# A fused embedding, sequence-filter and attention kernel: small loads behind the text rows, normed rows on two 64-partition sections, projections on both, bias added by VectorE

## The reference

```python
h = tok(x, W)                       # edge pad, patches of 16 with step 8, rfft, product with W.T
h = concat([h, txt(x_txt, ...)])    # 1024 + 77 = 1101 rows: tree embedding looked up by x_txt
h = h + attn(layernorm(h), ...)     # "attn": a long convolution over the rows, gelu, W_fc, gelu, + input, layernorm
h = h + ffn(layernorm(h), ...)      # below
# ffn, 4 heads n, 4 experts e, head dimension 16
sx = x @ hl_w[n].T + hl_b[n]                       # (b, 4, rows, 16)
q = sx @ wq[n, e].T;  k = sx @ wk[n].T;  v = sx @ wv[n].T
att = softmax(q @ k.T * 4 + causal);  out = att @ v
mixed = sum_e(out[e] * softmax_e(out @ gate_w + gate_b))
hn = layernorm(mixed + sx[n, n])
fout = layernorm(fc2(relu(fc1(hn))) + hn)          # inside each head
return fout * softmax_n(fout @ fgate_w.T)
```

## Time and profile before

| what | value |
|---|---|
| median of 3 runs | 1377.04 us (1374.37 to 1379.66) |
| the profiled execution's own time | 1382.09 us |
| its span, first to last instruction | 1379.2 us |
| mean granted TensorE clock | 0.893 |
| busy share of the span: PE, DVE, ACT, POOL | 79%, 57%, 55%, 32% |
| front stage, from the span's start | 0 to 186 us |
| sequence stage | 186 to 373 us |
| first prologue | 373 to 442 us |
| period 0 | 442 to 565 us |
| six full periods, period 7, last epilogue | 565 to 1221, to 1320, to 1379 us |

### The profile page before, as it was taken

One profiled execution on the slowest core, in us unless ns is written; L12 is line 12 of the kernel. 1 busy time (PEld: TensorE's weight loads), 2 busy tenths in 40 slices (PEclk: granted clock), 3 DMA queues, 4 the chain that ended last, 5 costly groups with the idle time before them and its releaser, 6 DMA issues.

```text
span 1379.2 us, 39174 instructions
## 1 busy us (share of the span) xinstructions
PE 1091.8 (79%) x15223; PEld 596.9 (43%) x15223; DVE 793.0 (57%) x1493; ACT 754.5 (55%) x906; POOL 443.6 (32%) x616
## 2 busy tenths in 40 slices
PE   3898628889052699989989889879989898989931
PEld 2455327775021345444444444444434444534411
DVE  3828675325756274267567558448567656752453
ACT  0242114452001565867867877866876786789820
POOL 3000031001520431243543543525444435355431
PEclk9999859995555798999999999999999999999965
DMA  8999049940406507404603612620830740550000
GB/s 147 214 170 240 11 104 202 203 79 1 103 21 116 76 15 138 65 4 109 108 9 99 109 19 78 99 53 15 152 60 15 135 77 14 113 91 3 3 17 10
DMA packets 114013, 113.69 MB, mean 82 GB/s; under 512 B 68072, under 2 KB 85239, under 8 KB 113669
## 3 DMA queue, kind: packets, MB, share of 16 engines
q1 hardware_dynamic: 109776, 110.59, 42.3%
q10 hardware_dynamic: 3733, 0.60, 0.3%
q0 software_dynamic: 320, 0.04, 0.0%
HBM read 88.07 MB, written 22.95 MB: 81 GB/s over the span
## 4 chain that ended last, share of the span: by engine, by line
PE 42%; issue 11%; ACT 9%; DVE 6%; POOL 3%; ACTq 0%; DMA 0%; POOLq 0%; DVEq 0%; SPq 0%
PE b_pso L1986 15%; PE b_pss L1950 13%; ACT b_pb L2065 9%; PE b_psm L2012 4%; PE b_pss L1948 3%; POOL b_pb L2103 2%; PE b_psm L2008 2%; PE b_psm L2029 2%; POOL b_stat L2084 1%; DVE b_rq L2191 1%; PE b_psm L1932 1%; DVE b_ks L2189 1%; PE b_psm L2033 1%; DVE b_squares L2190 1%; PE b_psm L2034 1%
## 5 line engine op out<-in xcount | busy, mean ns | idle before, releaser
L2065 ACT ACTIVATE b_pb<-b_pss 128x1024 f32<-128x1024 f32 (+2 forms) x736 | 648.4, 940 | 295.7 <-PE b_pss L1950 221.7
L1986 PE MATMUL b_pso<-b_pb,b_vop 128*32 128x128 f32 (+4 forms) x4800 | 407.3, 415 | 28.6 <-POOL b_pb L2103 28.5
L2103 POOL TENSOR_SCALAR_AFFINE_SELECT b_pb<-b_pb 128x256 f32<-128x256 f32 (+1 forms) x544 | 253.4, 487 | 495.5 <-ACT b_pb L2065 492.6
L1950 PE MATMUL b_pss<-b_qop,b_kop 97*32 97x512 bf16 (+3 forms) x6144 | 354.4, 333 | 52.3 <-issue 31.0
L1950 PEld LDWEIGHTS b_pss<-b_qop,b_kop 97*32 97x32 bf16 x6144 | 140.3, 96 | 274.9 <-ACT b_pb L2065 156.0
L1986 PEld LDWEIGHTS b_pso<-b_pb,b_vop 128*32 128x32 f32 x4800 | 159.7, 112 | 109.9 <-issue 39.5
L2279 DVE STREAM_TRANSPOSE b_ot<-b_pso 128x512 f32<-128x512 f32 x64 | 45.9, 717 | 133.5 <-PE b_pso L1986 131.1
L2084 POOL TENSOR_TENSOR b_stat<-b_stat,b_mh 128x18 f32<-128x18 f32 x34 | 110.2, 3259 | 30.2 <-DVE b_stat L2358 18.8
L920 PE MATMUL psc<-tz,ub 128*64 128x128 f32 x1152 | 79.8, 283 | 16.2 <-ACT tz L961 8.8
L920 PEld LDWEIGHTS psc<-tz,ub 128*64 128x64 f32 x1152 | 71.5, 141 | 24.5 <-ACT tz L961 12.7
L2012 PE MATMUL b_psm<-b_xt,w_all 65*128 65x384 f32 x144 | 63.4, 562 | 18.9 <-DVE b_rq L2191 16.4
(11 more groups left out here) (394 smaller groups left out, 1308.9 us busy)
## 6 DMA issues: line engine op xcount, KB each, us to landing
b_qop<-qk_parts_b SPq DMA_DIRECT2D x192, 144.0 KB
tz<-taps SPq DMA_DIRECT2D x64, 304.0 KB, 9.6
x<-in_x SPq DMA_DIRECT2D x16, 1024.0 KB, 14.6
qk_parts_b<-b_qs SPq DMA_DIRECT2D x16, 864.0 KB, 5.3
b_kop<-qk_parts_b SPq DMA_DIRECT2D x192, 36.0 KB
qk_parts_b<-b_ks SPq DMA_DIRECT2D x8, 432.0 KB, 3.9
n_late<-id_d SPq DMA_DIRECT2D x1, 2400.0 KB, 9.4
h<-z SPq DMA_DIRECT2D x8, 288.0 KB, 2.8
```

Source lines behind the costliest of these rows:

```text
L1950: mm = pe.matmul(pss[VW * g:VW * g + VW, u % 2, b, col:col + w], lhs, qop[:, n, e, q0:q0 + w], start=True, stop=True, skip_group_check=True)
L1986: mm = pe.matmul(acc, vop[0:P if j < NA - 1 else LAST, j, n, :], rhs, start=(j == 0), stop=(q0 == P * j if x < 2 else j == NA - 1), skip_g ...
L2065: nc.scalar.activation(pb[:, SLOT[un], 0:nb, 0:w], pss[:, s % 2, 0:nb, 0:w], ACT.Exp, scale=float(HD) ** 0.5).then_inc(exped, 1)
L2103: ins = pool.affine_select(out=v_, in_=v_, compare_op=ALU.is_ge, fill=0.0, base=0, pattern=pat, channel_multiplier=-1)
```

## The change

1. **Front, SP's queue.** The 32 small loads L303 and L308 are issued behind the text rows and behind the store of the taps.
2. **Sequence stage.** The copy `ul` moves from POOL to ScalarE. POOL's addition to `hh` waits until the convolution is over (`psw_out` 3). `w_all` gets 128 rows: its 64 weight rows twice (from `whad`, wha's columns twice). The bias row becomes two tiles, `vb` (v and residual bias in every partition, made by TensorE with `whab`) and `bcol` (q and k bias by column), copied by VectorE. The gate product moves to the fifth of the 16 groups; the wait for the last group moves behind the first bias matmul.
3. **FFN, two sections.** `xt` is [128, 576]: positions 0 to 575 on partitions 0 to 63, 576 to 1151 on 64 to 127. Each product is a pair of matmuls with 64 contracted rows, one on each half of the array's rows, into different banks. "feat" becomes 6 jobs of 2 x 288 positions instead of 5 (of them one half job) with 9 x 384; "tok" and "rmat" are 8 blocks of 128 and two of 64. VectorE adds the bias as it takes a job out. A prologue has 10 jobs instead of 9, and FULL_STEPS (VectorE's steps in a full period) is 96 instead of 87.
4. **Slots.** PRO, EPI, XNORM, CHECK and BOUND get the slots in the diff: the norm of the next rows stands at slot 0 instead of 9, its turn at 11 instead of 21.
5. **First prologue.** `run(-1)` uses three PSUM areas in turn, so TensorE may be two jobs ahead of VectorE; "tok" is last. The k parts of head 0 are copied back by ScalarE's queue, as soon as k is spilled; `run(0)` starts scores when all jobs of it are given free.
6. **End.** The flag is computed during the last epilogue and stored before the last output.

```diff
@@ front, SP @@
                 small_weights()
-                gate_weights()
...
                 sp.dma_start(krev_d, kr).then_inc(kr_stored, 16)
+                block_weights()
+                gate_weights()
@@ sequence stage @@
+                pe.matmul(psf[:, 1, 0:NH * VC], whad[:], w.wvx[:].rearrange("p n c -> p (n c)"), start=True, stop=True)
+                pe.matmul(psf[:, 1, NH * VC:2 * NH * VC], whab[:], w.wvx[:].rearrange("p n c -> p (n c)"), start=True, stop=True)
...
-                pool.tensor_copy(ul[:], ut[:].rearrange("p d a b -> p (a b) d")).then_inc(ul_ok, 1)
-                pool.wait_ge(ul_ok, 1)
+                pool.wait_ge(psw_out, 3)
                 pool.tensor_tensor(hh[:], hh[:], bmid(w.lnb[:], NG), ALU.add).then_inc(hl_ok, 1)
@@ FFN stage @@
+        PRO = [(11, "turn", 0), (15, "tok", 0), (19, "feat", (2, 0)), (24, "feat", (2, 1)), (30, "knorm", 0), (33, "feat", (0, 0)), (37, "feat", (0, 1))]
+        PRO += [(41, "feat", (1, 0)), (46, "feat", (1, 1)), (50, "qnorm", 0)]
+        EPI = [(55, "fc1", 0), (58, "fc2", 0), (61, "back", 0), (64, "back", 1)]
...
-        CHECK, BOUND = 25, 51
-        FXNORM, XNORM, LASTNORM = (11, (28, 31), 36), (9, (11,), 14), (71, (74, 76), 80)
+        CHECK, BOUND = 17, 53
+        FXNORM, XNORM, LASTNORM = (11, (28, 31), 36), (0, (5,), 8), (71, (74, 76), 80)
+        FIRST = [(11, "turn", 0)] + [j for j in PRO if j[1] not in ("turn", "tok")] + [(56, "tok", 0)]
+        def area(p, i):
+            return (psm[:], pss[:, 0], pss[:, 1])[i % 3] if is_first(p) else psm[:]
@@ SP, ACT: first prologue @@
+                        if not att:
+                            sp.wait_ge(keys_out, 1)
...
+                    if not att and pro:
+                        act.wait_ge(spilled, 32)
+                        act.sem_inc(keys_out, 1)
+                        for i, kp in enumerate(TERMS_K):
+                            act.dma_start(kop[HD * i:HD * i + HD, 0], qk_d[0, kp, 2 * P:2 * P + HD]).then_inc(placed[0], 16)
@@ PE, fill @@
                     elif kind == "feat":
-                        gate(base)
-                        for i, (g, x) in enumerate(c):
-                            mm = pe.matmul(psm[:, i, 0:FB], wall[:, g * P:g * P + P], xt[:, x * FB:(x + 1) * FB], start=True, stop=True)
+                        psm = gate(base, p, kind)
+                        g, i = c
+                        for h in range(2):
+                            r = slice(D * h, D * h + D)
+                            mm = pe.matmul(psm[:, h, 0:PIECE], wall[r, g * P:g * P + P], xt[r, PIECE * i:PIECE * i + PIECE], start=True, stop=True)
@@ DVE, empty, a q job (FEAT) @@
-                        ch.step(cp(dst(0), psm[0:m, 0:z, 0:FB]))
-                        ch.step(tt(squares[0:m, slot[c[0]]:slot[c[0]] + z, :], dst(0), dst(0), ALU.mult))
-                        give(tt(rq[0:m, 0:z], psm[0:m, 0:z, 0:FB], dst(0), ALU.subtract))
+                            ch.step(ts(dst(0), psm[:, :, 0:PIECE], bcol[:, g:g + 1], None, ALU.add))
+                            ch.step(tt(cut(sqq[:, g, :]), dst(0), dst(0), ALU.mult))
+                            give(stt(rest, psm[:, :, 0:PIECE], bcol[:, g:g + 1], dst(0), ALU.add, ALU.subtract))
@@ DVE, norms @@
                         if att and not prev and s == RNORM[2]:
-                            v.wait_ge(rstd, roots0 + 2)
+                            v.wait_ge(rstd, roots0 + 3)
```

More of the change, by code:

```diff
@@ L1705, in stage_ffn_bounded @@
     UB, PB, LAG = 2, 5, 3
+    HALF, PIECE = LP // 2, LP // 4
+    MIDDLE = NA // 2
+    BLOCKS = [(a + 5 * h, h, P * (a + 5 * h) - HALF * h, P, 0) for a in range(MIDDLE) for h in range(2)]
+    BLOCKS += [(MIDDLE, 0, P * MIDDLE, P // 2, 0), (MIDDLE, 1, 0, P // 2, P // 2)]
     units = score_units(UB, whole_tiles=True)
@@ L1845, in _, with copies @@
                     sp.sem_inc(s_, c)
-                def copies(c, n):
+                def copies(c, n, keys=True):
                     qk, mt_ = qk_d[c], mt_d[c]
@@ L1921, in job, with gate, turn_rows @@
                     k[0] += 1
-                def gate(base):
-                    pe.wait_ge(free, base + k[0] + 1)
-                def turn_rows(src, base):
-                    gate(base)
+                def gate(base, p, kind):
+                    if is_first(p):
+                        need = {"turn": 1, "feat": 2, "tok": 2, "knorm": 4, "qnorm": k[0] + 1}[kind]
+                        pe.wait_ge(free, max(need, k[0] - 1))
+                    else:
+                        pe.wait_ge(free, base + k[0] + 1)
+                    return area(p, k[0])
+                def turn_rows(src, base, p, kind):
+                    psm = gate(base, p, kind)
                     pe.sem_inc(passed, 1)
@@ L1996, in fill @@
                         pe.wait_ge(rn_ok, 1)
-                        turn_rows(h4[:, NA * c:NA * (c + 1)], base)
+                        turn_rows(h4[:, NA * c:NA * (c + 1)], base, p, kind)
                         return
                     if kind == "rmat":
-                        gate(base)
-                        for a in range(NA):
-                            mm = pe.matmul(psm[:, 0, a * HD:(a + 1) * HD], xt[:, a * P:(a + 1) * P], wall[:, WC + HD * c:WC + HD * c + HD], start=True, stop=True)
+                        psm = gate(base, p, kind)
@@ new lines, in fill @@
+                        for a, h, c0, n, off in BLOCKS:
+                            r = slice(D * h, D * h + D)
+                            if n == P:
+                                o = NH * VC * (a % 5)
+                                mm = pe.matmul(psm[:, h, o:o + NH * VC], xt[r, c0:c0 + n], wall[r, WV:], start=True, stop=True)
+                            else:
+                                for z in range(2):
+                                    mm = pe.matmul(psm[off:off + n, z, 4 * NH * VC:TOK], xt[r, c0:c0 + n], wall[r, WV + NH * VC // 2 * z:WV + NH * VC // 2 * (z + 1)], start=True, stop=True)
+                    elif kind == "feat":
+                        psm = gate(base, p, kind)
+                        g, i = c
+                        for h in range(2):
+                            r = slice(D * h, D * h + D)
+                            mm = pe.matmul(psm[:, h, 0:PIECE], wall[r, g * P:g * P + P], xt[r, PIECE * i:PIECE * i + PIECE], start=True, stop=True)
@@ L2041, in run @@
                         pe.wait_ge(late_ok, 2)
+                        pe.wait_ge(free, len(PRO) + 1)
                     for s in range(SPAN):
@@ L2115, in run @@
                                 root(variances(p) + norms, st, i * m, (i + 1) * m)
+                        if not att and prev and s == REDUCE:
+                            pool.wait_ge(flag_ready, 1)
+                            pool.partition_all_reduce(bad[:, 1:2], bad[:, 0:1], channels=P, reduce_op=RMAX).then_inc(bad_ready, 1)
                     if not att and not prev:
@@ L2196, in empty @@
-                        if c == ((2, 2),):
-                            ch.step(red(nearest[D:P, 3:4], nearest[D:P, 0:4], AX.X, ALU.min))
+                            rest = rq[0:D]
+                            give(ts(rq[:], psm[:, :, 0:PIECE], bcol[:, 2:3], None, ALU.add))
+                            v.wait_ge(free, base + k[0] + 1)
+                            if i == 0:
+                                ch.done(red(nearest[D:P, 0:2], rq[D:P], AX.X, ALU.min, apply_absolute_value=True))
+                            else:
+                                ch.done(red(nearest[D:P, 2:3], rq[D:P, 0], AX.X, ALU.min, apply_absolute_value=True))
+                                ch.done(red(nearest[D:P, 3:4], rq[D:P, 1, 0:L - 3 * PIECE], AX.X, ALU.min, apply_absolute_value=True))
```

184 lines of the change are left out of this document (109 added, 75 removed).

## The result

The changed kernel takes 1320.78 us, median of 4 runs (1311.28 to 1330.65), against 1377.53 for the one before in the same comparison: ratio 0.959 with a 95% interval of 0.9505 to 0.9676, so 56.8 us or 4.1% faster. The forecast was 1333.5 (-43.6), in a range of 1314 to 1358. Two later comparisons gave 1319.06 (ratio 0.9558, 0.9514 to 0.9601) and 1317.99 (0.9534, 0.9503 to 0.9565). The profiled execution took 1314.63, its span is 1312.2; against the 1379.2 of before that is -67.0, more than the medians show: the profiled execution of before took 4.6 us more than its median, that of the changed kernel 6.2 less.

The account below looks back on a forecast made before the run. Limits taken: late text rows (front), DMA (convolution), a TensorE-VectorE chain (first prologue), TensorE (full periods). Terms -7.7 - 2.9 - 0.5 - 12.5 + 7.5 - 27 - 0.5 = -43.6 gave 1333.5 us, range 1314 to 1358.

Parts of the forecast that it names:

- Rival 4: Period 0: no stall, since TensorE runs ahead with scores and full tiles; 1321 us, chance 10%.
- Front, convolution, fold: Text rows issued earlier, -7.7 us; taps arriving steadily, -2.9; gate product off the path between fold and W_fc, -0.5.
- First prologue: Three areas leave only VectorE's part, q ready 10.8 us earlier; fewer key copies on SP's queue, 1.7; sum -12.5.
- Scores start near 429.7: End of the first prologue: first scores at 429.7 instead of 442.26.
- Pairs: Full periods: both halves run together, a feat job 0.75 us instead of 1.49, tok 1.45 instead of 2.42.
- rival 1: Feat, tok, rmat: halves don't run together, feat pair 1.2 us, tok 2.3; +22 and +6 us, 1361, chance 8%.
- Rival 2: Tok and rmat: only the loads go in turn, tok saves 0.3 us instead of 0.95; +7, 1340.5, chance 10%.
- +7.5: Period 0, net us: late rows and residual norm stall TensorE; shorter rmat (3.2) and feat, tok, waits (4.0) come off.
- The +13.0: Period 0: masks behind POOL's roots go on 41.1 us after the first scores instead of 28.1.
- Full periods: Six periods: shorter feat and tok, less waiting for POOL, minus 1.3 us at the turn; -4.5 each, -27 in all.
- Rivals 3 and 5: Full periods: (3) VectorE's slot-0 wait holds TensorE, 1395 us, 4%; (5) `xn` 2 to 3 us after slot 11, 1348, 13%.
- The end: Tail: flag arithmetic, POOL's reduction and the last DMA leave it, -0.5 us.

Follow-up runs that it names:

- the variant on one half: Changed kernel with both matmuls of every feat, tok and rmat pair contracting rows 0 to 63, so they cannot run side by side: 1352.98 us in one run.

## Why the prediction was right or wrong

The time lies in the range, 12.7 us under the forecast of 1333.5. In the profile the kernel gained 23.4 us more than the sum has: 10.7 of it in period 0, 9.3 in the W_fc products and 5.0 in the full periods, with the other parts 1.6 the other way. Rival 4 names the very time (1321 for 1320.78), but its mechanism is not there: the stall came, so that agreement is luck.

**Front, convolution, fold: right in the profile, less sure than it looks.** -7.15, -2.9 and -0.7 for -7.7, -2.9 and -0.5. Undoing the order of the small loads brings the 7.7 us wait back. But the front takes 178.9 to 182.4 us in the 12 profiles that have the new order, 4.7 to 8.2 less than the one profile of before, and the convolution 103.6 to 105.6 in all 13 profiles with the change, 1.7 to 3.7 less. No run undoes the changes to the convolution by themselves. ScalarE's copy of `ul` took 8.55 us, above the 4 to 8 of the forecast.

**First prologue: right in size, the cause named wrong.** -12.7 for -12.5 (-11.7 to -12.7 in the three profiles), and the keys' queue gives about 2 where the sum had 1.7. VectorE's part is as forecast, 3.5 us for a q job (379.89 to 383.38) where the sum had 3.3. But "with three areas only VectorE's part stays" names the wrong cause: with one area only 2 to 3 us come back. What is left, some 8 us, can only be put down to "tok" going last and pairs of 1.33 us at half clock instead of jobs of 2.92, which fit into VectorE's own time. That is argued, not shown: no run undoes either. "Scores start near 429.7" counts the prologue alone; with the front and the sequence stage the same sum gives 418.7. They started at 409.46, 32.8 us earlier than before where the signs had 23 to 25, and 9.3 of that are the W_fc products.

**Pairs: right.** 0.69 and 1.46 us for 0.75 and 1.45, and the variant on one half shows that it is the halves: 1.17 and 2.35, as rival 1 had (1.2 and 2.3). Rival 1 would have cost more than forecast, though: that variant is 38 us longer in its span than the second profile of the changed kernel (1350.9 to 1312.8), not 28. Rival 2 is out with "tok" at 1.46: 16 loads of 128 columns and 8 of 64 start within it. An estimate by what the Trainium skill, "TensorE: Matmul & The Clock Gate", section "LDWEIGHTS (loading the stationary operand)", gives for one load puts them at 2.1 us one after another. That fits the 2.35 of the variant on one half and not the 1.46 on two, so on different rows they overlap.

**Period 0: a stall, but on another path and of another size, and the sum wrong.** The step that failed is "**+7.5**", in three places. First the path. The +13.0 is the time by which POOL's masks go on later (41.1 for 28.1), and POOL's roots did end there, at 449.93, 40.5 us after the first scores. But TensorE did not wait for the masks. Its longest wait in the first 20 slots, in the changed kernel and then in the one before:

```profile
PE b_psm L1976 <- DVE b_xn L2417: 21.1, 1, 21.1
```

```profile
PE b_pso L1986 <- POOL b_pb L2103: 8.1, 1, 8.1
```

TensorE stood at the turn, now in slot 11, for `xn`, which came 34.5 us after the first scores; no wait for POOL is on its list for period 0. Second the size. At slot 20 period 0 was 14.2 us behind the one before, close to the +14.7 of the sum, but by luck: 4.6 of it are the turn, "tok" and the first "feat" (2.44, 1.46 and 0.69 us on TensorE), which stand ahead of slot 20 now and stood behind it before. The stall itself cost 9.6. Third, from slot 20 to its end the period won 17.4 us: 3.6 in the four "rmat" jobs (0.89 each for 0.8), 7.1 in the other jobs (2.5 net of the 4.6 moved ahead, where the sum had 4.0), and an estimated 6.8 by the clock, which the sum did not hold. Windows of the kernel before, around its first two "rmat" jobs (at 523.0 and 532.2), then of the changed one around its own:

```profile
520.00:525.00 5.00, 5.00 (x52) 3.43 (x50) 2.13 (x3) 2.49 (x3) 0.00 (x0) 1.00 0.52 176
525.00:529.00 4.00, 4.00 (x34) 1.23 (x33) 0.31 (x1) 1.94 (x2) 0.00 (x0) 0.57 0.53 126
529.00:535.00 6.00, 6.00 (x76) 4.10 (x76) 4.31 (x12) 3.07 (x3) 0.81 (x2) 1.00 1.05 129
535.00:539.00 4.00, 4.00 (x48) 1.53 (x40) 0.04 (x1) 2.99 (x4) 1.53 (x4) 0.57 1.04 127
```

```profile
496.00:500.00 4.00, 4.00 (x57) 1.95 (x54) 2.16 (x9) 2.83 (x4) 0.00 (x0) 1.00 0.04 9
503.00:507.00 4.00, 4.00 (x84) 2.56 (x84) 3.44 (x14) 2.70 (x3) 1.58 (x4) 1.00 1.05 130
```

Before, the clock went to half for 3.4 us behind each of the four (525.1, 535.3, 545.6, 555.8), some 1.7 us lost each time, 6.8 in all; in the profile with the shorter jobs it stays up. That it is the length of "rmat" fits the variant on one half, where jobs of 2.11 us again have three such drops (508.7, 525.7, 536.0); the changed kernel has none in one profile and one in each of two others. It is not isolated: that variant makes "feat" and "tok" longer too. The row for period 0 showed a clock of 0.86, and the forecast did not ask what it was made of.

**Full periods: mechanism right, 0.8 us each too small.** -5.3 for -4.5. The jobs gave 3.6 (forecast 3.25). The wait for POOL's masks fell by 2.3 a period (1.8 forecast), the waits for ScalarE grew by 2.2, which the sum did not have, and the 1.3 at the turn did not come (0.2). Before there were six drops of 3.4 us in the six periods, in the changed profile one of 6.8: some 1.1 us a period, again the term that was missing.

**W_fc products: not in the sum at all.** -9.3 in the profile, by a clock that fell 22 us into them instead of 3. The moved gate product has part in it, but it is not all: by their mean clock, 4 of 14 runs seem to go without the gain.

**Rivals 3 and 5** did not cost anything. The sign for rival 3 is there, VectorE waits up to 6.3 us for `b_hb` in full periods, but TensorE does not wait with it; the turn waits 0.2 us in the period shown and 1.0 in all six. **The end** gained nothing (+0.6 for -0.5).

## What to carry to other kernels

Before summing what shorter jobs save, look up the granted clock of each stretch in the row of its window, and ask which jobs the dips follow: here the clock was worth some 6.8 us in period 0, 1.1 in each full period and 9.3 in the W_fc products, and no term of the sum had it. When work is moved ahead of a wait in a hand-written order, check the one period in which that wait is long: putting the residual norm back ahead of `b_hb` gave 9 to 11 us in period 0, and issuing the load earlier 9 more. When two places of a program are compared, count the work that the change moved across them. And jobs that two engines share need the slower one's time between them: with jobs three slots apart a full period was 111.9 us, with four or five 104.6.
